# Three units of maxima instead of two beside each of the last twelve tiles of the projection

## The reference, cut to what matters

```
xn = layernorm(x)
attention: qkv = xn @ W_qkv + b_qkv           (4, 1024, 768)
           reshaped to 16 heads x 1024 rows x 48, split into q, k, v of 16 each
           softmax(causal(q k^T / sqrt(512))) v, then @ W_out + b_out
feed-forward: light_out for every token; s = xn . routing_token;
           50 iterations of coordinate descent on s for each batch,
           the best 256 tokens of a batch pass the heavy block
out = x + attention + feed-forward
```

## Time and profile before

| what | value |
|---|---|
| median of three runs | 727.79 us (726.37 to 729.85) |
| the profiled execution's own time | 727.58 us |
| its span, first to last instruction | 725.9 us |
| mean granted TensorE clock | 0.983 |
| busy: PE, DVE, ACT, POOL | 673.3, 552.7, 403.6, 380.2 us |
| projection with units beside it, tiles 20 to 31 | about 87.1 to 135.1 us of the span |
| main loop | about 135.1 to 592 us |
| output projection, choice, heavy block | about 592 to 725.9 us |

### The profile page before, as it was taken

The page is one execution under the profiler, slowest core; times in us unless marked ns, Lnnn a source line. Parts: engine busy times, 40 slices in busy tenths (PEclk is TensorE's granted clock), DMA queues, the critical chain, the costliest instruction groups (busy, mean ns, idle before and its releaser), DMA issues. The chain is left out here.

```text
span 725.9 us, 12455 instructions
## 1 busy us (share of the span) xinstructions
PE 673.3 (93%) x3987; PEld 295.4 (41%) x3987; DVE 552.7 (76%) x1565; ACT 403.6 (56%) x908; POOL 380.2 (52%) x774
## 2 busy tenths in 40 slices
PE   4977999899999997999999999999999999778996
PEld 2643545323333332333333333333333358664745
DVE  4854877899999999999999999999996324643301
ACT  2421221478787783876778777776776753222140
POOL 5678200358676877488677554355453332246203
PEclk9999999999999997999999999999999999999999
DMA  8999866469689589587993664653930515661112
GB/s 276 211 217 221 204 204 189 117 135 143 124 124 181 99 148 154 95 160 128 137 176 61 122 95 56 88 102 48 183 45 8 130 15 190 201 190 58 17 13 30
DMA packets 247057, 92.49 MB, mean 127 GB/s; under 512 B 212992, under 2 KB 232608, under 8 KB 243872
## 3 DMA queue, kind: packets, MB, share of 16 engines
q1 hardware_dynamic: 245456, 89.60, 61.6%
q0 software_dynamic: 1536, 2.10, 1.8%
HBM read 56.65 MB, written 35.01 MB: 126 GB/s over the span
## 5 line engine op out<-in xcount | busy, mean ns | idle before, releaser
L1252 DVE CUSTOM_DVE_ANT_0 ps<-ps,maskrow 128x640 f32<-128x640 f32 (+7 forms) x512 | 374.8, 780 | 26.0 <-PE ps L999 24.3
L871 ACT ACTIVATE strips<-ps 128x512 f32<-128x512 f32 (+1 forms) x608 | 311.2, 577 | 103.6 <-PE ps L1025 91.3
L999 PE MATMUL ps<-QTk,QTq 96*128 96x512 bf16 (+3 forms) x768 | 188.4, 336 | 18.4 <-DVE mx L1252 15.3
L1025 PE MATMUL ps<-QTq,QTk 99*128 99x512 bf16 (+3 forms) x768 | 185.1, 330 | 1.1 <-DMA QTq<-m_d 0.5
L1043 PE MATMUL ps<-strips,vext 128*32 128x512 f32 (+3 forms) x1536 | 162.2, 497 | 0.0
L999 PEld LDWEIGHTS ps<-QTk,QTq 96*128 96x128 bf16 x768 | 51.7, 98 | 173.0 <-DVE mx L1252 150.2
L1025 PEld LDWEIGHTS ps<-QTq,QTk 99*128 99x128 bf16 x768 | 67.6, 98 | 89.9 <-ACT strips L871 44.7
L967 PE MATMUL ps<-shared,xrT 128*128 128x384 f32 (+1 forms) x256 | 96.4, 510 | 5.1 <-DVE shared L1219 5.0
L1677 POOL TENSOR_SCALAR_AFFINE_SELECT strips<-strips 128x512 f32<-128x512 f32 x128 | 79.1, 634 | 36.9 <-ACT strips L871 36.4
L1252 DVE DVE_READ_ACCUMULATOR2_ANT mx<- 128x1 f32 x512 | 72.3, 141 | 0.0
L967 PEld LDWEIGHTS ps<-shared,xrT 128*128 128x128 f32 x256 | 48.0, 198 | 32.6 <-issue 9.3
(11 more groups left out here) (145 smaller groups left out, 680.4 us busy)
## 6 DMA issues: line engine op xcount, KB each, us to landing
qkv_d<-shared SPq DMA_DIRECT2D x32, 384.0 KB, 3.7
pieces_d<-pieces SPq DMA_DIRECT2D x64, 192.0 KB, 3.4
qk<-qkv_d SPq DMA_DIRECT2D x64, 128.0 KB, 3.9
QTq<-pieces_d SPq DMA_DIRECT2D x16, 384.0 KB, 5.1
QTk<-pieces_d SPq DMA_DIRECT2D x16, 384.0 KB, 7.6
vext<-qkv_d SPq DMA_DIRECT2D x16, 256.0 KB, 5.7
QTq<-pieces_d SPq DMA_DIRECT2D x16, 256.0 KB, 5.6
QTk<-pieces_d SPq DMA_DIRECT2D x16, 256.0 KB, 8.4
```

What stands on the lines that cost most here:

```text
L871: nc.scalar.activation(dst, src, ACT.Exp, scale=SCALE).then_inc(exp_done, 1)
L999: mm = pe.matmul(psM[:, s, at:at + n], QTq[0:W, f % 3, c * 1024 + qb * P:c * 1024 + (qb + 1) * P], QTk[0:W, f % 3, c * 1024 + k0:c * 1024 ...
L1025: mm = pe.matmul(psE[:, (NE * q + j) % ES, k * n:(k + 1) * n], QTk[0:W + 3, q % 3, c * 1024 + kb * P:c * 1024 + (kb + 1) * P], QTq[0:W + 3 ...
L1252: ins = nc.vector.tensor_tensor_reduce(scores, scores, maskrow[:, 1024 - n:1024], 1.0, MASKED, ALU.add, ALU.max, mx[:, f % 2, 8 * c + qb:8 ...
```

## The change

Twelve more units are moved out of the main loop to the projection: BEGUN goes from 12 to 24, so FIRST holds all units of steps 0 and 1. Tiles 14 to 19 keep two units each; tiles 20 to 31 get three. The third unit is issued by PE after the second half of the projection, and reduced by DVE after the second. The maxima of step 0 are then complete at tile 24, so their transpose, store and load each come two tiles earlier. Four constants of the planner are set anew, so the order of the main loop is planned anew. The planner is also told that the units of FIRST are done at its start.

```
-EARLY, BEGUN = 3, 12
+EARLY, BEGUN = 3, 24
-STEP, PACE = 27.53, 31.86
-SOON, LATER, BEHIND = 0.19, 11.5, 1.84
+STEP, PACE = 27.23, 31.49
+SOON, LATER, BEHIND = 0.19, 8.0, 2.05
...
+    for x in FIRST:
+        done["Vector", x] = 0.0
...
-        return 12.09 * PACE
+        return 12.06 * PACE
...
-    BESIDE = {FRONT_FROM + k: FIRST[2 * k:2 * k + 2] for k in range(NT - FRONT_FROM)}
-    FIRST_DONE = FRONT_FROM + 2 * NU
+    THREE_FROM = 20
+    BESIDE = {t: FIRST[2 * (t - FRONT_FROM):2 * (t - FRONT_FROM) + 2] for t in range(FRONT_FROM, THREE_FROM)}
+    for t in range(THREE_FROM, NT):
+        at = 2 * (THREE_FROM - FRONT_FROM) + 3 * (t - THREE_FROM)
+        BESIDE[t] = FIRST[at:at + 3]
+    FIRST_DONE = THREE_FROM + (4 * NU - 2 * (THREE_FROM - FRONT_FROM)) // 3
...
                 for h in range(2):
                     ring_item(items[h])
                     project(t // 2, t % 2, h)
+                for x in items[2:]:
+                    ring_item(x)
...
                     if t > FRONT_FROM:
                         evacuate((t - 1) // 2, (t - 1) % 2)
-                    _, f, c, u = BESIDE[t][1]
-                    largest(f, c, u)
+                    for _, f, c, u in BESIDE[t][1:]:
+                        largest(f, c, u)
```

## The result

| | kernel before | changed kernel |
|---|---|---|
| median | 728.17 us (four runs) | 744.38 us (four runs) |
| the profiled execution's own time | 727.58 us | 745.21 us |
| its span | 725.9 us | 743.4 us |
| mean granted TensorE clock | 0.983 | 0.974 |
| projection, tile 20's first unit to the loop's first matmul | 48.05 us | 65.3 us |

The change makes the kernel slower: ratio 1.0212, 95% interval 1.0171 to 1.0254. The predicted 738.7 us was 5.7 us too low; 744.38 lies in the full range (730 to 746), but outside the 735 to 742 that were given for the forecast's own case. One of the four executions took 1595.33 us, as one of the kernel before beside a later run took 2254.1, and is left out of the ratio; the others took 742.02, 743.56 and 745.21, with a median of 743.56.

What follows compares the result with a forecast made beforehand. DVE was taken to pace the main loop's units, and one PSUM slot the projection with three units: 727.6 + 17.1 (projection) - 6.0 (loop) = 738.7 us. Range 735 to 742 for this case, 730 to 746 in full.

Steps and rivals of the forecast that it cites:

- The projection: Beside tiles 20 to 31, three units through one PSUM slot make tiles of 5.16 and 5.55 us; stage grows 17.1 us.
- The waits for stores at nothing: In the projection, four waits for stores of tiles (3.0 us before) cost nothing; if back, 3 us are added.
- The clock: In the projection, PE's gaps of a few tenths to 1.3 us in each tile leave the clock high, 2.4 GHz.
- rival 3: The clock oscillates beside the projection, some 2.5 us a tile in four tiles of twelve: 749 us; chance 0.08.
- The loop's gain: Main loop loses twelve units, but step 3 waits for its operands: 6.0 us gained, far ends 0 and 14.5.
- They can start at once: gain up to 3.1: Step 0's scores, formerly begun 3.1 us into the loop, start at once since their maxima load two tiles earlier.
- With fewer units between them perhaps 1 to 3 us: Step 0's scores, 24.7 us long before, get 1 to 3 us shorter with fewer units between them.
- step 3 starts: Step 3's units start just when their operands land, 38.9 us into the loop against 44.3 before.
- DVE therefore sets the pace of the units: Main loop while units are left: DVE busy 361.1 of 376.3 us, 27.8 us in a step of 28.9.
- rivals 1 and 4: Main loop: rival 1, operands don't bind, all 14.5 gained, 730.2 (0.15); rival 4, DVE's idle 15.2 goes too, 715.0 (0.08).
- While DVE sets the pace they are worth nothing: In the main loop, the some 5 us of matmuls that PE loses gain no time.
- Rival 2: The loop gives nothing, step 3's load comes as late as before: 744.7 us, up to 747.7; chance 0.14.

Runs made afterwards that it cites:

- e1: Changed kernel's projection with three units beside tiles 20 to 31, but the main loop of the kernel before, so twelve units are made twice: 747.07 us.
- e5: Changed kernel with three units only beside tiles 26 to 31, so six units leave the loop, same planner constants: 742.58 us.
- e7: Changed kernel with DVE's evacuation of a tile cut in halves, one before the second reduction, one before the third: 738.48 us.
- e8: Changed kernel with two PSUM slots for the units beside the projection, units cut into single blocks, transposes in one bank: 728.99 us.
- e9: Changed kernel, but in the main loop DVE reduces only 512 of the 1024 columns of a last block of rows: 739.04 us.
- e6: Changed kernel with step 3 working on step 0's operands, so its own load and the wait for it are gone: 741.21 us.
- e10: Changed kernel, but from step 3's second pair PE leaves out the second 512 columns of a last block of rows: 738.85 us.

## Why the prediction was right or wrong

**The projection: right, step by step.** 65.2 us were summed and 65.3 measured, 17.1 and 17.25 for the growth; both kinds of tile fit to 0.01 us, which is better than the estimates in the sum (0.60, 1.13 and 1.14 us) could promise. e1 shows that it is all on the path, e5 that it goes by the number of tiles, e7 that half an evacuation out of the chain is worth what the chain says, e8 that a second slot takes the loss away.

**The waits for stores at nothing: right.** They don't appear in the changed kernel; in e8, at 4.0 us a tile, 2.6 us of them come back.

**The clock: right by the rows.** The granted clock was 1.00 in the whole stage with PE gaps of 1.03 and 1.15 us in each tile. The rule of the Trainium skill ("TensorE: Matmul & The Clock Gate", the section on PSUM-queue depth-cycling) that was weighed is not borne out in this stage; rival 3 is out. At the loop's start and inside it the clock did fall (last section).

**The loop's gain: right in sign, mis-sized.** 6.0 us were forecast, 2.3 measured (456.9 to 454.6). "They can start at once: gain up to 3.1" brought 0.2, since the order has three units and a transpose first. "With fewer units between them perhaps 1 to 3 us" brought 2.5: step 0's scores took 22.2 us (156.41 to 178.6) in place of 24.7. The load of step 3 was issued at once, without another ahead of it (179.29), and its last part landed 6.8 us after its issue in place of 9.9. So the operands were there 37.3 us into the loop, 6.5 earlier than before (43.8): nearly the 6.0 of the forecast, by another split, which is partly luck. What failed is "step 3 starts" when they land: the order kept PE on other work for 3.8 us more, so the unit came only 3.1 us earlier, and 0.8 of them were lost behind it.

**The view of the loop under it was wrong as well:** "DVE therefore sets the pace of the units", from which "14.5 us at most" and rivals 1 and 4 came. DVE is busy 96% there, but e9 took 25 us of work from it and its 13 steps got 2.6 us shorter, part of it by the clock. "While DVE sets the pace they are worth nothing", said of PE's matmuls, came near the truth but for another reason: at full clock, work taken from either engine brought next to nothing in this order. e6 points the same way: with the load gone, the binding that the prediction named, 3.7 us are gained at most, and not the 8 or more that DVE as the limit would have given.

**The rest of the gap.** 727.6 + 17.25 - 2.3 = 742.5 for the profiled execution, whose own time is 745.21. The missing 2.6 are the 1.05 us by which tile 20 began later, the 1.4 behind the loop, and rounding. They came from stretches that the change doesn't touch; the runs have 132.1 to 135.5 us behind the loop. Rival 2, "the loop gives nothing", had 744.7, closest of all to the median of 744.38; but the loop did give 2.3 us, and it is these 2.6 that hide it. That the numbers agree is chance.

**Still open.** What sets the pace of the main loop is not shown. It is neither DVE's nor PE's amount of work alone. A chain of waits between the engines in the planned order (for slots, for exponentials, for the masks) would fit, but these were not varied one by one. The fall of the clock was not controlled, so the loops of single profiled executions can't be compared to better than some 4 us. And no constants were searched for e5 or e8, so a better order may exist for either.

## What to carry to other kernels

Work moved into a stage with room on both engines is not free if all of it goes through one buffer: then the time is the sum of producing, reducing and handing over, however idle both engines look. Walk that chain from the timeline before moving work, and give it a second buffer before giving it more work. And of two engines that are both busy over 95%, the shares don't tell whether either one sets the pace. Take a known amount from each in turn, and compare the runs piece by piece between the same events, with the clock beside them: here the whole-loop numbers pointed to PE, and the pieces showed a fall of the clock.

## What the runs showed of the hardware that was not expected

The clock at the loop's start. Before, PE waited 1.24 us for the last evacuation, and the granted clock from 135.1 to 178.6 was 0.96. In the changed kernel the wait is 2.36 us, and the clock was at its lower level (1.2 GHz) for nearly all of the next stretch, though PE was busy in it:

```profile
150.00:155.00 5.00, 1.78 (x8) 0.44 (x7) 4.35 (x14) 0.39 (x1) 0.00 (x0) 1.00 0.33 136
155.00:162.00 7.00, 6.85 (x21) 2.65 (x21) 5.44 (x15) 4.54 (x10) 5.89 (x4) 0.51 0.59 96
162.00:165.00 3.00, 3.00 (x23) 1.13 (x21) 3.00 (x7) 2.67 (x7) 2.35 (x6) 1.00 0.65 142
```

The gaps of 1.03 and 1.15 us in each tile before it had not done this. What it costs was not measured by itself; step 0's scores, which began in it, were still faster than before.

The clock inside the loop. With the new order PE comes to short gaps near 265 us. Here are the changed kernel (first two rows) and e10 (last two):

```profile
265.98 1.08 PE L1005 MATMUL ps<-QTk,QTq 96*128 96x384 bf16 x4 [1.22 <-DVE mx L1260]
267.90 0.82 PE L1005 MATMUL ps<-QTk,QTq 96*128 96x512 bf16 x2 [0.84 <-DVE mx L1260]
...
264.30 1.07 PE L1005 MATMUL ps<-QTk,QTq 96*128 96x384 bf16 x4 [1.22 <-DVE mx L1260]
266.21 0.50 PE L1005 MATMUL ps<-QTk,QTq 96*128 96x512 bf16 x2 [0.84 <-DVE mx L1260]
```

After them the granted clock was 0.53 from 267 to 278 us in the changed kernel, and 1.00 throughout in e10. It was also low for 7 us in e7, whose loop is the changed kernel's (gaps of 1.22, 0.85 and 0.81 us). So gaps of this size have been followed by a fall of 11 us, of 7 us and by none. Whether e10's missing matmuls had a part in that is not shown, but the clock differs between executions of e10 too: its two fastest, 734.74 us and the profiled 735.43, had mean clocks of 0.990 and 0.985, and its five of 739.8 to 740.8 us had 0.978 and 0.979. The step in which it fell took 29.9 us, against 26.1 without: 3.8 us, as much as many of the differences that the experiments looked for.
